# First layer norm of a fused attention and feed-forward block: applied on transposed data, with its factors spread through DRAM

## The reference

```python
mod = (silu(c) @ wmod).reshape(8, 6, 1, 128)
sa, ca, ga, sb, cb, gb = (mod[:, n] for n in range(6))
ga, gb = (sign(g) * max(abs(g), 0.25) for g in (ga, gb))

h = layernorm(x) * (1 + ca) + sa             # the FIRST norm: what the change is about
x = x + ga * attn(h)                         # retention: 8 heads, rotary, decay, causal, head norm, silu gate, Wo
h = layernorm(x) * (1 + cb) + sb             # the second norm
x = x + gb * ffn(h)                          # token shift, sigmoid(xr Wr) * (relu(xk Wk)^2 Wv)

def layernorm(x, eps=1e-5):                  # over the 128 channels of a token
    return (x - mean(x)) / sqrt(var(x) + eps)
```

## Time and profile before

| | |
|---|---|
| median of three runs | 750.47 us |
| the profiled execution | 750.22 us, span 748.4 us |
| TensorE busy | 737.4 us (99%), granted clock 1.000 |
| VectorE busy | 600.5 us (80%) |
| GpSimd busy | 589.0 us (79%) |
| ScalarE busy | 490.2 us (65%) |
| DMA | 25.67 MB, mean 34 GB/s |
| chain that ended last | 92% TensorE |

### The profile page before, as it was taken

How to read it: one execution, slowest core, us unless ns; L and a number is a source line. 1 busy time by engine, 2 the same in 40 slices (tenths; PEclk the granted TensorE clock), 3 DMA queues, 4 the chain that set the end, 5 groups by cost and what they waited for, 6 DMA issues and landing times.

```text
span 748.4 us, 29033 instructions
## 1 busy us (share of the span) xinstructions
PE 737.4 (99%) x12159; PEld 648.3 (87%) x12159; DVE 600.5 (80%) x1265; ACT 490.2 (65%) x956; POOL 589.0 (79%) x643
## 2 busy tenths in 40 slices
PE   8989999999999999999999999999999999999997
PEld 7778888888988888888888988888888988988886
DVE  4997787978788787987879798797987878787546
ACT  4566667676675766767666666756667576656665
POOL 6877788888789887898878888788877988787641
PEclk9999999999999999999999999999999999999999
DMA  6611000001011010111102011020111101001100
GB/s 249 193 31 19 13 17 17 16 18 31 12 27 39 10 44 16 24 37 31 31 10 51 16 24 32 13 48 17 28 26 31 34 14 31 16 9 31 24 16 28
DMA packets 56161, 25.67 MB, mean 34 GB/s; under 512 B 36184, under 2 KB 53856, under 8 KB 56032
## 3 DMA queue, kind: packets, MB, share of 16 engines
q1 hardware_dynamic: 55312, 23.02, 12.9%
q10 hardware_dynamic: 720, 0.80, 0.3%
HBM read 11.22 MB, written 4.20 MB: 21 GB/s over the span
## 4 chain that ended last, share of the span: by engine, by line
PE 92%; DVE 3%; ACT 1%; issue 1%; DMA 1%; POOL 1%; SPq 0%; DVEq 0%
PE ring L309 52%; PE outs L309 15%; PE O_E L309 14%; PE ring L324 8%; PE O_O L309 3%; PE ring L374 2%; DMA N<-in_w_vT 1%; ACT y L771 0%; DVE N L1097 0%; DVE rot_k L1060 0%; DVE A L1070 0%; DVE qT L1031 0%; DVE sin_k L1063 0%; POOL gn_rstd L1383 0%; DVE ln_stats L1004 0%
## 5 line engine op out<-in xcount | busy, mean ns | idle before, releaser
L1390 POOL TENSOR_TENSOR y<-y,gate 128x512 f32<-128x512 f32 x120 | 154.8, 1308 | 29.5 <-ACT y L771 29.5
L735 ACT ACTIVATE v<-ring 64x512 f32<-64x512 f32 x128 | 75.9, 593 | 85.6 <-PE ring L309 84.8
L1373 POOL TENSOR_TENSOR rot_k<-rot_k,sin_k 128x256 f32<-128x256 f32 x128 | 106.8, 856 | 24.1 <-DVE sin_k L1063 24.1
L309 PEld LDWEIGHTS outs<-wo_gated,y 128*128 128x128 f32 x992 | 119.7, 192 | 5.1 <-DVE y L1136 0.5
L309 PE MATMUL outs<-wo_gated,y 128*128 128x128 f32 x992 | 121.7, 275 | 0.1
L1090 DVE TENSOR_REDUCE gn_sum<-N 128x4 f32<-128x512 f32 x118 | 75.5, 681 | 42.4 <-ACT N L759 42.4
L1383 POOL TENSOR_TENSOR gn_rstd<-gn_var,minus_half 128x8 f32<-128x8 f32 x64 | 105.3, 1645 | 5.0
L1070 DVE TENSOR_TENSOR A<-ring,consts 128x256 f32<-128x256 f32 x128 | 47.9, 415 | 60.1 <-PE ring L309 60.1
L771 ACT ACTIVATE y<-ring,gn 128x512 f32<-128x512 f32 x126 | 90.8, 775 | 5.2 <-PE ring L324 5.2
L1367 POOL TENSOR_TENSOR qT<-qT,swapped 128x512 f32<-128x512 f32 x60 | 76.9, 1282 | 18.1 <-DVE swapped L1046 17.8
L743 ACT ACTIVATE kT<-ring 128x512 f32<-128x512 f32 x64 | 38.2, 597 | 80.1 <-PE ring L324 80.1
(11 more groups left out here) (193 smaller groups left out, 2100.8 us busy)
## 6 DMA issues: line engine op xcount, KB each, us to landing
k_odd<-rot_k SPq DMA_DIRECT2D x128, 64.0 KB, 2.4
X<-in_x SPq DMA_DIRECT2D x16, 256.0 KB, 3.9
out<-X SPq DMA_DIRECT2D x15, 256.0 KB, 2.5
key_tables<-in_const SPq DMA_DIRECT2D x7, 256.0 KB, 5.5
rotary_q<-in_const_q SPq DMA_DIRECT2D x2, 512.0 KB, 6.4
gates<-stored_rows SPq DMA_DIRECT2D x8, 128.0 KB, 3.2
N<-in_w_qkT SPq DMA_DIRECT2D x1, 512.0 KB, 5.1
N<-in_w_vT SPq DMA_DIRECT2D x1, 512.0 KB, 6.3
```

The lines of the kernel that those rows point to most:

```text
L309: return e.matmul(o, lhsT, rhs, start=start, stop=stop, skip_group_check=True)
L735: done = e.activation(v[halves(half), i % 2, 1, :, :], by(PAIRS, bank_of["v", odd, i][halves(1 - half), :]), ACT.Copy)
L1373: done = e.tensor_tensor(turned[:, n, :, :], turned[:, n, :, :], sin[:, n, :, :], op)
L1390: e.tensor_tensor(y[:, n % NY, :], y[:, n % NY, :], gate[:, n % 2, :], ALU.mult).then_inc(sem["y"])
```

## The change

From group 3 on (`BY_ROWS = 3`) the first norm is applied on data that arrives transposed. The host also passes x as `xT`, channels by tokens.

- ScalarE issues a DMA that writes r and -m*r of the group, [128 x 8] numbers, to a small DRAM tensor `written_rows`, so that they lie there as two rows of 512 (`write_rows`, step 4g - 11).
- SP issues a DMA that reads these two rows into all 128 partitions of `row_of`, 512 KB (`spread_rows`), and one that loads the group's columns of `xT` into `x_turned`, 256 KB (`load_turned`), both at SP's step 4g - 60, behind a load of x and ahead of `swap_k`.
- ScalarE makes (1 + ca) * row + sa of the second row (`scale_rows`, step 4g - 8). VectorE computes x_turned * (1 + ca) * row (`apply_rows`, step 4g - 6). GpSimd adds the two into `h_full` (`add_rows`, step 4g - 8). Rounding and splitting stay.
- Gone for these 13 groups: `norm_apply(g, 0)`, `transpose_n(g, 0)` with its bank, `full_h(g)`.
- Moved: `norm_stats(g, 0)` two steps earlier (4g - 10), `norm_rstd(g, 0)` two steps earlier (4g - 13), `load_x` two steps earlier.
- Several semaphores are merged to make room (weights, gn and mu, the late key tables).

```diff
-        ln_rstd = sb("ln_rstd", [P, 2, GC])
-        ln_shift = sb("ln_shift", [P, 2, GC])
+        ln_rows = sb("ln_rows", [P, 2, 2, GC])
+        ln_rstd, ln_shift = ln_rows[:, :, 0, :], ln_rows[:, :, 1, :]
+        row_of = sb("row_of", [P, 2, W])
+        x_turned = sb("x_turned", [P, W])
...
+        written_rows = nc.dram_tensor("written_rows", (2, 2, W), F32, kind="Internal").ap()
...
@@ TensorE
-                for g in due(step + 5, GC, NGROUP, 3):
-                    transpose_n(g, 0)
...
@@ ScalarE
                 at.wait_ge(f"ln_shift{which}", g + 1)
-                at.wait_ge("n0T", min(g + NORM_AHEAD, NGROUP) if which else g)
+                at.wait_ge("n0T", min(g + NORM_AHEAD, BY_ROWS) if which else g)
...
+            def write_rows(g):
+                at.wait_ge("ln_shift0", g + 1)
+                e.dma_start(written_rows[g % 2].rearrange("k (j p) -> p (k j)", p=P), ln_rows[:, 0, :, :].rearrange("p k j -> p (k j)"),
+                            allow_slow_non_contiguous=True).then_inc(sem["rows_written"], 16)
+            def scale_rows(g):
+                b = g // GB
+                at.wait_ge("rows_read", 32 * (g - BY_ROWS + 1))
+                e.activation(row_of[:, 1, :], row_of[:, 1, :], ACT.Identity, bias=mod_cols[:, 0, b:b + 1],
+                             scale=mod_cols[:, 1, b:b + 1]).then_inc(sem["rows_scaled"])
...
-                for g in due(step + 7, GC, NGROUP, 3):
-                    norm_apply(g, 0)
+                for g in due(step + 11, GC, NGROUP, BY_ROWS):
+                    write_rows(g)
+                for g in due(step + 8, GC, NGROUP, BY_ROWS):
+                    scale_rows(g)
                 for g in due(step - 8, GC, LAST):
                     norm_apply(g, 1)
...
@@ VectorE
+            def apply_rows(g):
+                b = g // GB
+                at.wait_ge("rows_read", 32 * (g - BY_ROWS + 1))
+                at.wait_ge("hT_lo", g)
+                e.scalar_tensor_tensor(out=h_full[:, :], in0=x_turned[:, :], scalar=mod_cols[:, 1, b:b + 1], in1=row_of[:, 0, :],
+                                       op0=ALU.mult, op1=ALU.mult).then_inc(sem["rows_applied"])
...
-                for g in due(step + 8, GC, NGROUP, 4):
+                for g in due(step + 10, GC, NGROUP, 4):
                     norm_stats(g, 0)
...
                     norm_heads(i, 0)
-                for g in due(step + 5, GC, NGROUP, 3):
-                    full_h(g)
+                for g in due(step + 6, GC, NGROUP, BY_ROWS):
+                    apply_rows(g)
                 for i in due(step - 1, 1, NCHUNK, 4):
                     norm_heads(i, 1)
...
@@ GpSimd
+            def add_rows(g):
+                at.wait_ge("rows_applied", g - BY_ROWS + 1)
+                at.wait_ge("rows_scaled", g - BY_ROWS + 1)
+                e.tensor_tensor(h_full[:, :], h_full[:, :], row_of[:, 1, :], ALU.add).then_inc(sem["h_full"])
...
                     low_h(g)
+                for g in due(step + 8, GC, NGROUP, BY_ROWS):
+                    add_rows(g)
                 for i in due(step + 4, 1, NCHUNK, 7):
                     rotate_k(i)
...
-                for g in due(step + 11, GC, NGROUP, 4):
+                for g in due(step + 13, GC, NGROUP, 4):
                     norm_rstd(g, 0)
...
@@ SP
+            def load_turned(g):
+                at.wait_ge("rows_applied", g - BY_ROWS)
+                e.dma_start(x_turned[:, :], xT[:, g * W:(g + 1) * W]).then_inc(sem["rows_read"], 16)
+            def spread_rows(g):
+                at.wait_ge("rows_written", 16 * (g - BY_ROWS + 1))
+                at.wait_ge("h_full", g)
+                e.dma_start(row_of[:, :, :], written_rows[g % 2].unsqueeze(0).broadcast_to([P, 2, W])).then_inc(sem["rows_read"], 16)
...
-                for g in due(step + 62, GC, NGROUP, 7):
+                for g in due(step + 64, GC, NGROUP, 7):
                     load_x(g)
                 for g in due(step + 37, GC, LAST):
                     store(g)
+                for g in due(step + 60, GC, NGROUP, BY_ROWS):
+                    spread_rows(g)
+                for g in due(step + 60, GC, NGROUP, BY_ROWS):
+                    load_turned(g)
                 for i in due(step + 55, 1, NCHUNK, 4):
                     swap_k(i)
```

More of the change, by code:

```diff
@@ L39 @@
 NORM_AHEAD = 4
+BY_ROWS = 3
+EARLY_TABLES = 4
 SEMAPHORES = (
@@ L49 @@
     "ln_mv1", "ln_rstd0", "ln_rstd1", "ln_shift0", "ln_shift1", "ln_stats0", "ln_stats1", "ln_var0", "ln_var1",
-    "mix_k", "mix_k_hi", "mix_k_lo", "mix_r", "mod_cols", "mod_cols_psum", "mu", "n0T", "n1T", "nT_psum", "n_E",
+    "mix_k", "mix_k_hi", "mix_k_lo", "mix_r", "mod_cols", "mod_cols_psum", "n0T", "n1T", "nT_psum", "n_E",
     "n_O", "o", "out0", "out1", "out2", "out3", "out4", "out5", "out6", "out_head", "product", "proj_k",
-    "proj_q", "proj_v_E", "proj_v_O", "qT", "r_psum", "r_tanh", "relu", "residual", "rot_k", "scaled", "scores",
+    "proj_q", "proj_v_E", "proj_v_O", "qT", "r_psum", "r_tanh", "relu", "residual", "rot_k", "rows_applied", "rows_read", "rows_scaled", "rows_written", "scaled", "scores",
     "silu_c", "sin_k", "sin_q", "small_consts", "sq_E", "sq_O", "state", "sum_E", "sum_O",
-    "swapped", "tables0", "tables1", "tables2", "tables3", "tables4", "tables5", "tables6", "tables7", "v_E",
+    "swapped", "tables0", "tables1", "tables2", "tables3", "late_tables", "v_E",
     "v_O", "v_mean", "v_sum", "w_ffn", "w_g", "w_g_hi", "w_g_lo", "w_k_hi", "w_k_lo",
-    "w_mod", "w_o", "w_qk", "w_qk_hi", "w_qk_lo", "w_v", "w_v_centred", "w_v_hi", "w_partners_hi", "w_partners_lo", "w_v_lo", "wffn_v",
+    "w_mod", "w_qk", "w_qk_hi", "w_qk_lo", "w_v", "w_v_centred", "w_v_hi", "w_partners_hi", "w_partners_lo", "w_v_lo", "wffn_v",
     "wo_gated", "x0", "x1", "x2", "x3", "x4", "x5", "x6", "y", "zero_column",
@@ L85, in constants, with build @@
     return np.concatenate(parts, 1).astype(np.float32), rotary_q.astype(np.float32)
-def build(nc, x, cT, w_mod, w_qkT, w_gT, w_vT, w_oT, norm_wb, w_ffnT, ffn_mu, const, const_q, out):
+def build(nc, x, xT, cT, w_mod, w_qkT, w_gT, w_vT, w_oT, norm_wb, w_ffnT, ffn_mu, const, const_q, out):
     with ExitStack() as ctx:
@@ L257, in outs, with normed_by, tables @@
             return [banks[j // PJ][:, j, :] for j in range(GC)]
+        def normed_by(g, which):
+            return ("rows_written", 16 * (g - BY_ROWS)) if which == 0 and g > BY_ROWS else ("ln_apply%d" % which, GC * g)
         def gates_of(b):
             return "gates%d" % (b % 2), 16 * (b // 2 + 1)
+        def tables(c):
+            return ("tables%d" % c, 16) if c < EARLY_TABLES else ("late_tables", 16 * (CB - EARLY_TABLES))
         def loaded(g):
@@ L545, in project_r @@
                 bank = take_bank(("r", g), ("r_tanh", g + 1))
-                at.wait_ge("w_ffn", 16)
+                at.wait_ge("w_ffn", 32)
                 at.wait_ge("mix_r", g + 1)
@@ L711, in scale_norm @@
             def scale_norm():
[L712 removed]
+                at.wait_ge("gn_mu", 32)
                 e.activation(gn[:, 0, :], gn[:, 0, :], ACT.Copy, scale=float(np.sqrt(V))).then_inc(sem["gn_scale"])
@@ L855, in _ @@
             load_tables(0)
-            e.dma_start(gn[:, :, :], norm_wb).then_inc(sem["gn"], 16)
+            e.dma_start(gn[:, :, :], norm_wb).then_inc(sem["gn_mu"], 16)
             at.wait_ge("small_consts", 1)
@@ L1000, in norm_stats @@
                     at.wait_ge("residual", g + 1)
-                at.wait_ge(f"ln_apply{which}", GC * g)
+                at.wait_ge(*normed_by(g, which))
                 at.wait_ge(f"ln_shift{which}", g)
@@ L1049, in rotate_k @@
                 c, bank = i % CB, bank_of["k", i]
-                at.wait_ge("tables%d" % c, 16)
+                at.wait_ge(*tables(c))
                 at.wait_ge("proj_k", i + 1)
@@ L1106, in mix_shift_r @@
                 at.wait_ge("delta", g + 1)
-                at.wait_ge("mu", 16)
+                at.wait_ge("gn_mu", 32)
                 at.wait_ge("product", g)
@@ L1352, in gate_weights @@
                 at.wait_ge(*gates_of(b))
-                at.wait_ge("w_o", 16)
+                at.wait_ge("w_ffn", 32)
                 at.wait_ge("out_head", H * (GB * b - 1) + (half + 1) * PAIRS)
@@ L1591 @@
         "x": lay(a(L0_attn_x)),
+        "xT": lay(a(L0_attn_x).reshape(B * T, C).T),
         "cT": lay(a(L0_c).T),
```

15 lines of the change are left out of this document (7 added, 8 removed).

## The result

| | before | after |
|---|---|---|
| median of four runs each | 750.34 us | 835.71 us (831.25 to 839.6) |
| ratio, 95% interval | | 1.1134 (1.11 to 1.1167) |
| profiled execution, its own time | 750.22 us | 832.31 us |
| its span | 748.4 us | 830.5 us |

The change costs 85 us, 6.6 us for each of its 13 groups. I had forecast a gain of 4.

What follows compares the result with a forecast made beforehand. TensorE's packed queue was taken as the bound: 750.2 - 5.7 (transposes removed) + 1.0 (group 3's late rows) + 0.9 (ring) = 746.4 us. The range meant to hold 8 times in 10 was 743.8 to 753.5 us.

Steps and rivals of the forecast that it cites:

- the cost of `write_rows`: ScalarE's DMA issue, taken at 0.6 us; landing in group 3 taken at 3.3, at most 5; other groups have over 20.
- The transposes: TensorE's queue gets 0.44 us shorter per removed block of four, 5.7 us over 13 groups.
- the check by steps 51 and 59: TensorE's step 51, with a transpose block, lasts 10.75 us; step 59, without one, 10.31: again 0.44.
- The fourth rival: Each removed TensorE transpose is worth its listed 0.274 us: 14.2 us off, 736.0 us; chance 0.02.
- The rows come late: First rival: ScalarE's `scale_rows` waits for DMAs in every group and stalls TensorE; 1 us each gives 759; chance 0.17.
- My working for the spread: SP's read into all partitions: 0.8 us per 128 KB beyond a fixed part, up to 3.2 us for 512 KB.
- Group 3: Write, spread and x transposed land after `scale_rows(3)` is due; TensorE loses about 1.0 us once, bounds 0 to 3.
- The ring: PSUM banks reused sooner, behind `apply_rows`: TensorE stalls 0.6 us in step 11, some 0.3 in 12; 0.9, bounds 0 to 1.5.
- VectorE: `apply_rows` replaces `full_h`: 1.03 us for 0.81, +0.2 us per group; below 38 us of 45, so no bound.
- the second rival: GpSimd, 39.7 of 44.6 us busy, bounds some steps: 0.3 us in 13 groups is 4 us, 750.4; chance 0.13.

Runs made afterwards that it cites:

- e10: e6 with VectorE's `apply_rows` one step earlier, behind the rotation of k, and GpSimd's `add_rows` behind its rotation of k: 746.9 us, ratio 0.9953.
- e6: e5 with the PSUM banks handed out as in the kernel before: 751.11 us, ratio 1.0012.
- e5: e3 with `spread_rows` and `load_turned` in SP's step + 61 instead of + 60, ahead of one more `swap_k`: 751.44 us, ratio 1.0017.
- e3: The changed kernel with the factors turned by one TensorE transpose, copied out by ScalarE and written as 8 pieces of 512 bytes: 754.99 us, ratio 1.0062.
- e1: The changed kernel with the write as 128 pieces of 32 bytes, the numbers in another order in DRAM: 756.82 us, ratio 1.0087.
- e2: The kernel before plus one write per group of 1024 packed 4-byte pieces into DRAM that nobody reads: 824.4 us, ratio 1.0987.
- e12 to e17: The kernel before plus one unread DRAM write per group of 1024 pieces, spaced 8 to 64 bytes apart or 8 to 64 bytes large: ratios 0.9993 to 1.0001.
- e4: The changed kernel with its write issued by SP instead of ScalarE: 853.87 us, ratio 1.1381.

## Why the prediction was wrong

The chain of kernels shows where 89 us went. From 746.9 (e10) the price of the order on VectorE and GpSimd is 4.2 (e6, 751.1), of the banks 0.3 (e5, 751.4; within the noise of the two), of SP's order 3.6 (e3, 755.0), of e1 against e3 1.8 (756.8), and of the packed pieces 78.9 (835.7).

**The step that failed: the cost of `write_rows`.** I priced the write as one issue, "I allow 0.5 to 1.5 and take 0.6", and wrote of its 1024 pieces that "in all groups but the third the write has over 20 us, so the rule would cost there nothing". The issue was indeed cheap, 0.37 us, and in all groups but the third the numbers are there long before they are read. But the landing, which I took at 3.3 us with 5 as the most, came some 9 to 11 us after the issue. In group 3 that kept ScalarE waiting for 2.72 us, against 0.84 in e1. The larger error is in the question. I asked when the write would be done and who waits for that, and never what it does to an engine that has no part in it. It costs 5.7 us per group as measured alone (e2), 6.1 in the changed kernel (78.9 / 13). I had also written that no row of the trace shows such a DMA, and then left its range at three numbers of the same kind; with no row for it, the bounds were those of my imagination. Nothing in the trace of before could have given the size. What it had no row for deserved a wide upper end.

The Trainium skill, "DMA: Bandwidth & Descriptors", Rules for kernel authors, advises against just this (a strided last dimension is one descriptor per element; rearrange it), and I argued the advice away. The trace agrees on the count: 1040 packets for a write of 1024 numbers. Following it is worth 79 us here. But the number of descriptors is not what costs: e12 to e17 also have 1024 pieces per write and cost nothing that can be measured.

**The transposes.** "0.44 for the block" and the check by steps 51 and 59 hold for what is taken out, and the transposes are gone as foretold: 72 of 124 are left.

```profile
L389 PE MATMUL ring<-consts,normed 128*128 128x128 f32 x72 | 11.3, 275 | 0.8 <-DMA consts<-in_const 0.6
```
The fourth rival (274 ns each) did not come true: even e10 gains 3.4 us and not 14. But 5.7 us is what the removal offers, not what is left: the groups of four steps last 44.39 to 44.45 us in most of e10, against 44.61 and 44.76 before, which is 0.2 to 0.3 per group.

**The rows come late**, my first rival, happened in 7 groups and not in 13, for 3.6 us in all by e5 and not for 0.7 to 1 per group. The transfers were not what made them late. I had allowed 7.4 to 8.4 us from the issue of the load of x (193.6) to the landing of x transposed (201 to 202). In the changed kernel that stretch is 6.4 us in groups 6 and 7 alike (269.86 to 276.23 in group 7). What failed is that I took one group for all: in group 8 ScalarE arrives 7.6 us after SP's issue and waits for nothing, in group 7 it arrives 3.9 us after it and waits for 2.46. My working for the spread also had a slip, as 3.2 less 2.4 us is the price of 64 KB more and not of 128. The times from issue to landing:

```profile
row_of<-written_rows SPq DMA_DIRECT2D x13, 512.0 KB, 4.0
...
x_turned<-in_xT SPq DMA_DIRECT2D x13, 256.0 KB, 4.7
```

**Group 3**, which I charged 1.0 us for its late rows, lost nothing on TensorE without the packed write: steps 5 and 6 of e1 last 10.31 and 10.32 us. **The ring** I charged 0.9 us in steps 11 and 12. In e1 step 11 does last 0.77 us longer than before, but e6, with the banks of before, keeps 0.5 of that and e10 none. The step I named was right and its cause was mostly not.

**VectorE** is the second wrong step. "Below 38 us of 45 there is no bound here" is a share of the group, the very thing that the first paragraph of the prediction warns of. Of the earlier trace rows, `apply_rows` was priced at 1.03 and has a mean of 0.89 in the changed kernel, with a median of 0.75, but it went into the one step in four where VectorE has only 0.41 us to spare. Its neighbours also grew: the mean `mix_r` of the changed kernel lasts 1320 ns against 1030 in the earlier trace rows. The place counted for more than that, since in e10 `mix_r` is slower still.

```profile
L1145 DVE SCALAR_TENSOR_TENSOR mix_r<-delta,mu,h2T 128x512 f32<-128x512 f32 x15 | 19.8, 1320 | 1.8 <-POOL delta L1440 1.8
L1389 POOL TENSOR_TENSOR h_full<-h_full,row_of 128x512 f32<-128x512 f32 x13 | 19.2, 1474 | 0.6 <-DVE h_full L1052 0.6
L746 ACT ACTIVATE row_of<-row_of,mod_cols 128x512 f32<-128x512 f32 x13 | 10.6, 819 | 10.6 <-DMA x_turned<-in_xT 10.6
```

**GpSimd**, the second rival, did not become a bound. It carries 610 us in e10, which is the fastest of all. `add_rows` took 1.47 us against 1.29, `scale_rows` 0.82 against 0.63.

That e10 ends at 746.9, half a microsecond from the forecast, is no merit of the sum: 3.4 us of gain against my 5.7 less 1.9, by other terms.

## What to carry to other kernels

Price a new DMA by what it writes where, not only by when it lands: a shape that no row of the trace shows deserves a wide upper end and a run by itself, a kernel that is the unchanged one plus that single DMA. Look at when it lands, and not only at when its packets move. When an engine that is only 80% busy gets more work, look up the step in which the work stands, for an order written by hand has idle time in some steps and none in others. And when a hole named "issue" stands in the middle of identical matmuls, look for a DMA that is still on its way; here the order of the work was not to blame.

## What the hardware showed that I had not expected

A write into DRAM of 4-byte pieces, packed side by side by different partitions, lands some 8 to 11 us after its issue, though its packets have moved within some 3 us. TensorE stands still in between, most often from some 4 to 5 us after the issue and for 1.5 to 5.9 us in all. This came about on ScalarE's queue (e2) and on SP's (e4), and with nobody waiting for the write (e2). The same 1024 pieces 8, 16 or 64 bytes apart, or 8, 16 or 64 bytes large, cost nothing that can be measured (e12 to e17, ratios of 0.9993 to 1.0001).

TensorE's granted clock goes to its lower level (0.50) with such holes and stays there for several microseconds, in which matmuls take 0.63 us instead of 0.40. In the changed kernel TensorE is busy for 766.9 us, and in e1, with the same instructions and no holes, for 736.8. That makes 30 of the 79 us, more than a third.

A pass of VectorE over two SBUF inputs lasts 1.74 to 1.80 us instead of 0.75 to 0.94 when a GpSimd pass of 128x512 began just before it. The Trainium skill, "SBUF — State Buffer", section "SBUF: two separate sides", names the mechanism: such a VectorE instruction and a GpSimd instruction that reads SBUF exclude each other for the whole of whichever began first. The rows of e6 at 81.14 and of e10 at 213.44 agree: in both, VectorE ends 0.5 us after GpSimd does, a little less than its 0.75 us alone.
